# Layer 1's numerators from the symmetric scores with spread row maxima, and layer 1 closed in two halves

## The reference, cut to what matters

```
u    = h @ h.T / sqrt(384)                       # 512 x 512, symmetric
a    = softmax(u, axis=-1);  delta = a * adj
attn = delta / (delta.sum(-1) + 1e-10)
hl, hs, hr = h @ wl.T + bl, h @ ws.T + bs, h @ wr.T + br
ctx  = (attn*upper) @ hl + diag(attn)[:,None]*hs + (attn*lower) @ hr
h    = relu((ctx - mean(ctx)) / sqrt(var(ctx) + 1e-12) * g + beta)
```

## Time and profile before

| | |
|---|---|
| median of three executions | 1246.11 us |
| lowest, highest | 1244.65, 1246.17 us |
| the profiled execution | 1245.14 us |
| its span, first to last instruction | 1243.4 us |
| its granted TensorE clock, as a share of full speed | 0.997 |
| busy: TensorE, VectorE, GpSimd, ScalarE | 99%, 68%, 39%, 37% |

### The profile page before, as it was taken

The page is one execution under the profiler, slowest core; times in us unless marked ns, Lnnn a source line. Parts: engine busy times, 40 slices in busy tenths (PEclk is TensorE's granted clock), DMA queues, the critical chain, the costliest instruction groups (busy, mean ns, idle before and its releaser), DMA issues.

```text
span 1243.4 us, 18757 instructions
## 1 busy us (share of the span) xinstructions
PE 1226.6 (99%) x7338; PEld 1205.2 (97%) x7338; DVE 845.5 (68%) x1982; ACT 458.4 (37%) x853; POOL 488.0 (39%) x486
## 2 busy tenths in 40 slices
PE   8999999999999999999999999999999999999996
PEld 7999999999999999999999999999999999999996
DVE  5566885568855778557775577755777568765586
ACT  4344333334333343342343323434333433234331
POOL 3364333443433344334443334433344332444324
PEclk9999999999999999999999999999999999999998
DMA  9011230013210132001321013211222112221000
GB/s 325 25 54 57 89 110 2 34 60 103 93 34 2 60 111 85 35 1 60 111 85 35 8 66 97 86 34 35 65 72 85 35 35 77 70 76 35 1 27 26
DMA packets 45449, 77.63 MB, mean 62 GB/s; under 512 B 2608, under 2 KB 28208, under 8 KB 45360
## 3 DMA queue, kind: packets, MB, share of 16 engines
q1 hardware_dynamic: 45072, 76.03, 18.6%
q10 hardware_dynamic: 288, 0.39, 0.1%
HBM read 63.84 MB, written 12.58 MB: 61 GB/s over the span
## 4 chain that ended last, share of the span: by engine, by line
PE 96%; DVE 2%; ACT 1%; issue 1%; POOL 0%; DMA 0%; POOLq 0%; DVEq 0%
PE rot_ps L270 16%; PE rot_ps L271 16%; PE rot_ps L272 16%; PE u_ps L270 14%; PE u_ps L271 14%; PE u_ps L272 14%; PE rot_ps L337 3%; PE rot_ps L345 2%; PE u_ps L329 1%; DVE x_stats L546 0%; ACT x_norm L417 0%; DMA x_norm<-x_dram 0%; POOL rstd L868 0%; DVE proj L636 0%; DVE z L673 0%
## 5 line engine op out<-in xcount | busy, mean ns | idle before, releaser
L270 PE MATMUL rot_ps<-w_hi,ht_hi 128*128 128x384 f32 x1152 | 396.7, 344 | 0.4 <-DVE proj L636 0.4
L271 PE MATMUL rot_ps<-w_lo,ht_hi 128*128 128x384 f32 x1152 | 388.3, 337 | 0.0
L272 PE MATMUL rot_ps<-w_hi,ht_lo 128*128 128x384 f32 x1152 | 388.1, 337 | 0.0
L851 POOL TENSOR_TENSOR hw_lo<-proj,hw_hi 128x768 fp32r<-128x768 f32 x128 | 217.3, 1698 | 362.8 <-ACT hw_hi L460 362.8
L270 PEld LDWEIGHTS rot_ps<-w_hi,ht_hi 128*128 128x128 f32 x1152 | 216.4, 188 | 0.7 <-DVE proj L636 0.7
L271 PEld LDWEIGHTS rot_ps<-w_lo,ht_hi 128*128 128x128 f32 x1152 | 216.6, 188 | 0.0
L272 PEld LDWEIGHTS rot_ps<-w_hi,ht_lo 128*128 128x128 f32 x1152 | 216.0, 187 | 0.0
L636 DVE TENSOR_TENSOR proj<-rot_ps,bias 128x384 f32<-128x384 f32 x256 | 138.3, 550 | 55.5 <-PE rot_ps L272 55.0
L863 POOL TENSOR_TENSOR dg<-et_hi,tri 128x256 fp32r<-128x256 f32 x128 | 102.1, 797 | 183.9 <-PE u_ps L272 183.9
L460 ACT ACTIVATE hw_hi<-proj 128x768 fp32r<-128x768 f32 x128 | 108.4, 847 | 170.1 <-DVE proj L636 170.1
L442 ACT ACTIVATE u_off<-u_ps 128x384 f32<-128x384 f32 x64 | 28.0, 438 | 362.3 <-PE u_ps L272 362.3
(11 more groups left out here) (87 smaller groups left out, 2002.8 us busy)
## 6 DMA issues: line engine op xcount, KB each, us to landing
out_dram<-z SPq DMA_DIRECT2D x64, 192.0 KB, 1.9
x_norm<-x_dram SPq DMA_DIRECT2D x15, 768.0 KB, 4.5
adj_a<-adj_t_dram SPq DMA_DIRECT2D x8, 1024.0 KB, 5.4
adj_b<-adj_t_dram SPq DMA_DIRECT2D x8, 1024.0 KB, 5.4
adj_a<-adj_dram SPq DMA_DIRECT2D x8, 1024.0 KB, 5.3
adj_b<-adj_dram SPq DMA_DIRECT2D x8, 1024.0 KB, 5.5
x_a<-x_dram SPq DMA_DIRECT2D x8, 768.0 KB, 4.6
x_b<-x_dram SPq DMA_DIRECT2D x8, 768.0 KB, 4.7
```

The costliest lines, as they stand in the source:

```text
L270: pe.matmul(dst, a_hi, b_hi, start=first and m == 0, stop=False)
L271: pe.matmul(dst, a_hi, b_lo, start=False, stop=False)
L272: done = pe.matmul(dst, a_lo, b_hi, start=False, stop=last and m == n - 1)
L851: pool.tensor_tensor(hw_lo[:, t, :, 0:dim], proj[:, t % 2, :, :], hw_hi[:, t, :, 0:dim].bitcast(F32), ALU.subtract).then_inc(hw_lo_done, 1)
```

## The change

The row maxima of layer 1 are spread: TensorE transposes each column of `neg_max`, repeated 128 times, into a rotating bank (unit M, `spread_max`), so that bank holds, on every partition, minus the scaled maximum of row j at column j. ScalarE copies it to `m_rows` (`copy_max`, in the space of `u_off`). VectorE adds it to the scaled scores in PSUM (`shift_scores`), and the exponential of that, element (j, i) with the maximum of row i, is already the turned numerator, as the scores are symmetric. It is masked with `adj_t`, rounded from SBUF, and no E unit is left. The row sums, which the E path got as a side result of the exponential, come from an exponential of their own into `e_sb` (`row_sum`). The second load of the adjacency goes.

Unit order of layer 1: four P, M, the other eight P, then T. `den_done` and its fellows count two in a layer-1 step.

The end of a layer-1 step is written anew: after `finish(0)` VectorE waits for the `x_norm` load; after `finish(1)` rows 0 and 1 are closed (`half(0)`: denominators, variance, `centre`), their `affine` stands between `finish(2)` and `finish(3)`, then `half(1)`. The four `x_statistics` are spread over this. The last step of the last pair keeps its own ending.

```
     UNITS_0 = [("P", *p) for p in PROJ + SELF] + TURN
-    UNITS_1 = [("P", *p) for p in PROJ]
-    for t in range(TILES):
-        UNITS_1 += [("E", t), ("P", *SELF[t])]
-    UNITS_1 += TURN
+    UNITS_1 = [("P", *p) for p in PROJ[:4]] + [("M",)] + [("P", *p) for p in PROJ[4:] + SELF] + TURN
...
+        m_rows = u_off[:, 0:n_rows]
...
-                    sp.wait_ge(masked, at(it, g, TILES, FOUR))
-                    sp.dma_start(adj_sb[g][:, :, :], rows(adj, it * 2 + g)).then_inc(adj_loaded[g], 16)
...
-                def turn_e(i):
...
+                def spread_max():
+                    pe.wait_ge(max_done, at(it, s, TILES, N_E))
+                    wait_bank("M")
+                    for t in range(TILES):
+                        done = pe.transpose(bank(it, s, "M")[:, t * P:(t + 1) * P],
+                                            neg_max[:, t:t + 1].to_broadcast([P, P]), ident[:, :])
+                    done.then_inc(m_ready, 1)
...
                 def attend(i):
-                    if layer == 1:
-                        pe.wait_ge(et_lo_done, at(it, s, i + 1, FOUR))
-                    elif i == 0:
+                    if i == 0:
                         pe.wait_ge(et_lo_done, at(it, s, TILES, FOUR))
...
-                        act.wait_ge(max_done, at(it, s, t + 1, N_E))
-                        act.activation(u_ps[t][:, :], u_ps[t][:, :], ACT.Exp, bias=neg_max[:, t:t + 1],
-                                       scale=scale, accum_out=z_sum[:, s % 2, t:t + 1]).then_inc(exp_done, 1)
+                        act.wait_ge(shifted, at(it, s, t + 1, N_E))
+                        act.activation(u_ps[t][:, :], u_ps[t][:, :], ACT.Exp).then_inc(exp_done, 1)
+
+                def row_sum(t):
+                    act.wait_ge(max_done, at(it, s, t + 1, N_E))
+                    act.activation(e_sb[:, t, :], u_ps[t][:, :], ACT.Exp, bias=neg_max[:, t:t + 1],
+                                   scale=scale, accum_out=z_sum[:, s % 2, t:t + 1]).then_inc(row_sum_done, 1)
+
+                def copy_max():
+                    act.wait_ge(m_ready, at(it, s, 1, N_M))
+                    act.activation(m_rows, bank(it, s, "M")[:, :], ACT.Copy).then_inc(m_copied, 1)
...
+                    row_sum(0)
                     round_proj(0)
+                    row_sum(1)
+                    row_sum(2)
+                    row_sum(3)
+                    copy_max()
+                    exp(0)
                     exp(1)
+                    round_proj(1)
                     exp(2)
+                    round_e(0)
                     exp(3)
-                    round_proj(1)
+                    round_e(1)
                     if s == STEPS - 1 and not last:
                         x_normalise(it * 2 + 3, range(0, 2))
...
                 round_proj(2)
+                if layer == 1:
+                    round_e(2)
+                    round_e(3)
...
                 def e_low(i):
-                        dve.tensor_tensor(et_lo[:, :, cols],
-                                          bank(s, "E", i)[:, :].rearrange("p (j n) -> p j n", n=P),
-                                          et_hi[:, :, cols].bitcast(F32), ALU.subtract).then_inc(et_lo_done, 1)
+                    dve.tensor_tensor(et_lo[:, i, :], e_sb[:, i, :], et_hi[:, i, :].bitcast(F32),
+                                      ALU.subtract).then_inc(et_lo_done, 1)
+
+                def shift_scores(t):
+                    if t == 0:
+                        dve.wait_ge(m_copied, at(it, s, 1, N_M))
+                    dve.wait_ge(row_sum_done, at(it, s, t + 1, N_E))
+                    dve.scalar_tensor_tensor(out=u_ps[t][:, :], in0=u_ps[t][:, :], scalar=scale, in1=m_rows,
+                                             op0=ALU.mult, op1=ALU.add).then_inc(shifted, 1)
...
                     for t in range(1, TILES):
                         row_max(t)
+                    evacuate(1, 0)
+                    evacuate(1, 1)
+                    shift_scores(0)
+                    shift_scores(1)
+                    evacuate(2, 0)
+                    shift_scores(2)
+                    shift_scores(3)
                     mask(0)
-                    evacuate(1, 0)
+                    evacuate(2, 1)
                     mask(1)
-                    evacuate(1, 1)
                     mask(2)
-                    mask(3)
-                    evacuate(2, 0)
-                    for t in range(TILES):
-                        diagonal(t)
-                    evacuate(2, 1)
...
                 evacuate(3, 0)
+                if layer == 1:
+                    mask(3)
+                    e_low(0)
                 evacuate(3, 1)
+                if layer == 1:
+                    for t in range(1, TILES):
+                        e_low(t)
                 for t in range(TILES):
+                    evacuate(t, 2)
                     if layer == 1:
-                        e_low(t)
-                    evacuate(t, 2)
+                        diagonal(t)
...
+                finish(0)
+                if ahead is not None:
+                    dve.wait_ge(x_norm_loaded, (ahead - 1) * 16)
+                finish(1)
+                half(0)
+                if ahead is not None:
+                    x_statistics(0)
+                finish(2)
+                dve.wait_ge(rstd_done, at(it, s, 1, N_HALF))
+                affine(0)
+                affine(1)
+                if ahead is not None:
+                    x_statistics(1)
+                finish(3)
+                half(1)
+                add_x(0)
+                add_x(1)
+                if ahead is not None:
+                    x_statistics(2)
+                    x_statistics(3)
+                    dve.wait_ge(x_stats_done, (ahead - 1) * XS + TILES)
+                dve.wait_ge(rstd_done, at(it, s, 2, N_HALF))
+                affine(2)
+                affine(3)
+                if ahead is not None:
+                    x_variance(ahead)
+                add_x(2)
+                add_x(3)
                 if ahead is not None:
                     x_shift_of(ahead)
```

More of the change, by code:

```diff
@@ L56, in build_digcn @@
     N_E = (0, 0, 4, 4)
+    N_M = (0, 0, 1, 1)
+    N_HALF = (1, 1, 2, 2)
     N_Z = (4, 4, 0, 0)
@@ L179, in at, with place, bank @@
             return it * sum(per) + (sum(per[:s]) + count)
[L181 to L185, removed]
+        def place(it, s, unit):
+            return it * len(ALL_UNITS) + sum(len(ORDERS[r]) for r in range(s)) + ORDERS[s].index(unit)
+        def bank(it, s, *unit):
+            return rot_ps[place(it, s, unit) % ROT]
         def p_count(t, n):
@@ L292, in wait_bank @@
                 def wait_bank(*unit):
-                    k = place(s, unit) - ROT
-                    if k < 0 and first:
+                    k = place(it, s, unit) - ROT
+                    if k < 0:
                         return
-                    r, before = ALL_UNITS[k]
-                    turn = it if k >= 0 else it - 1
+                    turn, (r, before) = k // len(ALL_UNITS), ALL_UNITS[k % len(ALL_UNITS)]
                     if before[0] == "P":
@@ L303, in wait_bank @@
                     else:
-                        pe.wait_ge(et_lo_done, at(turn, r, before[1] + 1, FOUR))
+                        pe.wait_ge(m_copied, at(turn, r, 1, N_M))
                 def scores(t):
@@ L694, in finish @@
                                              op1=ALU.add).then_inc(c_freed, 1)
-                    if i > 0 and not final:
+                    if i > 0 and not final and not (layer == 1 and i == 2):
                         aggregate(i - 1)
@@ L772, in step @@
                     return
-                for i in range(TILES):
-                    finish(i)
-                    if layer == 1 and 0 < i < TILES - 1:
-                        dve.wait_ge(aggr_done, at(it, s, i, FOUR))
-                        centre(i - 1)
-                    if ahead is not None and i in (1, 2):
-                        if i == 1:
-                            dve.wait_ge(x_norm_loaded, (ahead - 1) * 16)
-                        x_statistics(2 * i - 2)
-                        x_statistics(2 * i - 1)
-                dve.wait_ge(stats_done, at(it, s, TILES, FOUR))
-                denominator(slice(0, TILES), 1)
-                aggregate(TILES - 1)
-                variance(slice(0, TILES), 1, TILES)
-                if ahead is not None:
-                    dve.wait_ge(x_stats_done, (ahead - 1) * XS + TILES)
-                    x_variance(ahead)
-                if layer == 0:
-                    dve.wait_ge(rstd_done, at(it, s, 1, ONE))
+                if layer == 0:
+                    for i in range(TILES):
+                        finish(i)
+                    dve.wait_ge(stats_done, at(it, s, TILES, FOUR))
+                    denominator(slice(0, TILES), 1)
+                    aggregate(TILES - 1)
+                    variance(slice(0, TILES), 1, TILES)
```

(21 more changed lines are left out.)

76 lines of the change are left out of this document (31 added, 45 removed).

## The result

The changed kernel takes 1275.86 us (median of 4 runs, 1275.07 to 1276.62) against 1246.14 for the kernel before on the same chip: ratio 1.0243, 95% interval 1.023 to 1.0256. It is 29.7 us slower, where +15.3 was forecast.

What follows compares the result with a forecast made beforehand. TensorE, busy 99% of the span, was taken as the bound. -20.4 removed work, +11.6 and +7.3 port losses, +16.8 M's wait gave +15.3 us on 1245.14: 1260.4 us, own range 1250 to 1268, overall range 1243 to 1268.

Steps and rivals of the forecast that it cites:

- 2.0 a step with M at 2.4: Upper end of the forecast's own range: 2.0 us of collisions a step and M waiting 2.4 us, given as 1268.
- Removed work: TensorE in layer 1: four E units removed, one M unit added at an E unit's price, 20.4 us less over 16 steps.
- M in step 2: TensorE's M unit in step 2: row maxima ready with 1.2 us to spare, nothing lost.
- M in step 3: M waits for late row maxima behind the moved x_norm wait: 2.4 us in 7 of 8 pairs, 16.8 us.
- the scores of the same step: Scores of step 3: finish(3) stays just in time for them; any cost there comes off M's wait.
- The port: Layer 1, before the turns: VectorE and GpSimd SBUF collisions make banks late, 1.45 us in step 2, 1.0 in step 3.
- rival (c): After M's wait, TensorE's lower clock slows four projections: 6.4 us each time, 45 in all, 1305 us; chance 0.05.
- Layer 0: Layer 0 after step 3: masks start 1.3 us later, banks met with 0.2 to spare; otherwise some 0.3 us per pair.

Runs made afterwards that it cites:

- a6: Changed kernel with the x_norm wait behind half(0), layer 1's masked numerators kept in PSUM, and x_variance moved before affine(2): 1222.84 us, ratio 0.982.
- a3: Changed kernel with layer 1's masked numerators kept in PSUM instead of SBUF, contexts also waiting for their diagonal: 1251.98 us, ratio 1.0057.
- a1: Changed kernel with VectorE's x_norm wait moved back behind finish(1) and half(0): 1248.32 us, ratio 1.0029.
- a2: Changed kernel with 12 extra matmuls, result overwritten, in step 3 in front of M's wait for the row maxima: 1268.16 us, ratio 1.0188.
- a8: Changed kernel with masked numerators in PSUM and 12 extra matmuls in front of M's wait in step 3: 1246.65 us, ratio 1.0009.

## Why the prediction was wrong

The direction and the waits forecast were right, the size was not: 29.7 us against 15.3, outside the range. The upper end of that range was also added up wrongly: 2.0 a step with M at 2.4 gives 1272 instead of 1268, which the measured time still exceeds.

**Removed work: right.** M costs what an E unit costs (in step 2 the projections start 0.36 us after M and lose 0.08 on their first matmul). Taking step 3 apart, some 1.3 us are gone from it, as forecast; a6 shows the sum, and 2 us beyond it.

**M in step 2: right.** No wait there.

**M in step 3: place, count and cause right, the size 3.1 instead of 2.4.** The 3.1 is an average over the seven pairs: 2.8 in front of M and 0.3 in front of the scores of the same step, which the text had called just in time, taking what they might cost out of M's wait. The landing came later than I had it. The last `h_low` of step 2 took 1.27 [the one at 433.43 above] instead of 0.72, and the load waits for it. The line of the kernel before, then the triangle on GpSimd that held it after the change:

```profile
424.38 0.72 DVE L647 TENSOR_TENSOR ht_lo<-x_norm,ht_hi 128x512 fp32r<-128x512 f32 x1 [0.64 <-ACT ht_hi L492]
```

```profile
433.41 0.74 POOL L898 TENSOR_TENSOR dg<-et_hi,tri 128x256 fp32r<-128x256 f32 x1 [2.60 <-PE u_ps L273]
```

They overlap in the same way in all pairs (`h_low` 1.26 to 1.27 against 0.71 to 0.73). I had let the late turns move contexts and landing by different amounts and overlooked that `h_low` and a triangle then collide. The closings took 0.26 more. Seven pairs x 0.7 = 5 us.

**The port: cause and place right, the sizes in part by luck.** Step 2 became 0.17 us longer (0.18 forecast), but its turns lost 1.6 instead of 1.45, and it ran 1.4 shorter without them (a3) instead of 1.27. In step 3 0.8 were lost in front of the turns (1.0 forecast); with the clock up, in a1 and a2, it is 1.2, so the slow matmuls gave VectorE time. The Trainium skill's sentence on the shared port (Advanced Engine Details and Errata, Mode Summary), if taken for its listed modes only, would have spared these subtractions; the earlier trace rows and a3 say that two SBUF inputs are enough.

**The step that failed: the forecast let TensorE stand still at no price but the time itself.** The clock stood as a rival (c) with 0.05, added to nothing. It happened in all seven pairs: from M to the first turn 14.6 us instead of 13.14, 1.45 a pair, 10 us in all. a1, a2 and a8 show that it goes when TensorE's idle time goes; a3 shows that idle time of that length does not bring it every time. As a rival it was mis-sized the other way: I let it last for all four projections, 6.4 us a pair; it lasted 3.4 us and cost 1.45. The Trainium skill (TensorE: Matmul & The Clock Gate, HAM oscillation) tells of idle gaps in front of matmuls that bring the lower level back; the trace agrees, with 0.50 granted behind all seven, while three of the seven in a3 were followed by 1.00.

**Layer 0: costed at nothing, 3 us.** Step 0 after such a step 3 is 0.45 longer. The view of waits has one wait of TensorE for a projection bank there, 0.45 in one pair. Some 0.3 of the average stands in a6 too, where layer 1 has no waits left, and steps of 37.03 and of 37.35 both occur in layer 0 of the kernel before; what makes them differ isn't shown. The text had named 0.3 a pair as the price if its 0.2 of slack was not there; that the number is near is no sign that this was the cause.

5 + 10 + 3 make 18 us; the waits in front of the turns came 0.2 a pair lower, 1.4 us, and steps 1 and the start 0.5 shorter. That leaves 16 for the difference of 16.2 between the span's 31.5 and the forecast's 15.3.

## What to carry to other kernels

In a kernel bound by one engine, look for the point at which every other engine meets it again, and count what stands in program order between the last outside event (here a load's landing) and that point: a wait moved over two calls put 2.9 us of work behind the landing and cost some 27 us. A stall of the bound engine must be priced with the clock that it gets back afterwards. And when an operand moves from PSUM to SBUF, ask who else wants two SBUF inputs at that time.

## What the runs showed of the hardware that was not expected

Idle stretches of TensorE of nearly the same length in front of M (2.6 to 3.0 us) were followed by the lower clock in all seven pairs of the changed kernel, and in four of seven with numerators in PSUM; the lengths of the two kinds overlap (2.58 to 2.97 and 2.59 to 2.65), and what decides between them isn't shown. Twelve matmuls with no use, put into the stretch, kept the clock up and made the changed kernel faster by 0.5 to 0.6%.
